# Adapter, layer norm and conditional linear on one core: the squares of the variance read the row sum, not the mean

## The reference

```python
h = relu(x @ W1[lang] + b1[lang])            # 512 -> 128
y = x + h @ W2[lang] + b2[lang]              # 128 -> 512, residual
mean = y.mean(-1); var = ((y - mean) ** 2).mean(-1)
n = (y - mean) * rsqrt(var + 1e-5)
x1 = x + n * gamma[lang] + beta[lang]
out = x1 + x1 @ W[cat] + b[cat]              # 512 -> 512
```

## Time and profile before

| | us |
|---|---|
| median of 3 runs | 620.67 |
| lowest and highest | 618.24, 621.05 |
| the profiled execution | 621.52 |
| its span, first to last instruction | 619.6 |
| PE, DVE, ACT, POOL busy in it | 610.4, 522.8, 510.6, 548.1 |
| granted TensorE clock | 1.000 of full speed |

### The profile page before, as it was taken

The page is one execution under the profiler, slowest core; times in us unless marked ns, Lnnn a source line. Parts: engine busy times, 40 slices in busy tenths (PEclk is TensorE's granted clock), DMA queues, the critical chain, the costliest instruction groups (busy, mean ns, idle before and its releaser), DMA issues.

```text
span 619.6 us, 10902 instructions
## 1 busy us (share of the span) xinstructions
PE 610.4 (99%) x2876; PEld 491.0 (79%) x2876; DVE 522.8 (84%) x1153; ACT 510.6 (82%) x769; POOL 548.1 (88%) x442
## 2 busy tenths in 40 slices
PE   9999999999999999999999999999999999999997
PEld 7667888887878787888787877877878887888786
DVE  1799898888998889898889888889898889898673
ACT  3768888889889889889889888888888889889770
POOL 3689999999999998999999999999999999999930
PEclk9999999999999999999999999999999999999999
DMA  8968998898998888988888997988988898897422
GB/s 299 236 205 277 312 302 286 250 294 261 308 299 272 269 281 268 312 276 295 263 295 261 305 300 246 286 286 270 307 295 274 274 297 253 302 303 264 163 85 103
DMA packets 125616, 166.25 MB, mean 268 GB/s; under 512 B 10866, under 2 KB 72316, under 8 KB 121488
## 3 DMA queue, kind: packets, MB, share of 16 engines
q1 hardware_dynamic: 94612, 150.12, 73.7%
q10 hardware_dynamic: 30972, 15.78, 9.0%
HBM read 132.17 MB, written 33.55 MB: 267 GB/s over the span
## 4 chain that ended last, share of the span: by engine, by line
PE 35%; POOL 29%; ACT 14%; issue 10%; DVE 6%; DMA 3%; SPq 2%; ACTq 1%; POOLq 0%; DVEq 0%
POOL xs_lo L375 8%; ACT norm L473 8%; POOL w_lo L402 7%; PE o_bank L807 7%; PE o_bank L805 6%; PE o_bank L806 6%; POOL x_tok L396 5%; POOL w_raw L386 3%; PE n_bank L823 3%; POOL w_lo L362 3%; DMA b_bc<-in_L_cond_b 2%; PE d_bank L836 2%; PE d_bank L805 2%; PE d_bank L807 2%; PE d_bank L806 2%
## 5 line engine op out<-in xcount | busy, mean ns | idle before, releaser
L805 PE MATMUL o_bank<-w_hi,x1T_hi 128*128 128x512 f32 x512 | 205.7, 402 | 0.9 <-DVE x1T_lo L706 0.8
L807 PE MATMUL o_bank<-w_hi,x1T_lo 128*128 128x512 f32 x512 | 200.5, 392 | 0.0
L806 PE MATMUL o_bank<-w_lo,x1T_hi 128*128 128x512 f32 x512 | 199.6, 390 | 0.0
L396 POOL TENSOR_TENSOR x_tok<-x_tok,b_bc 128x512 f32<-128x512 f32 x128 | 163.8, 1304 | 12.5 <-PE o_bank L885 7.6
L402 POOL TENSOR_TENSOR w_lo<-w_raw,w_hi 128x512 fp32r<-128x512 f32 x128 | 163.3, 1300 | 9.9 <-ACT w_hi L483 9.9
L473 ACT ACTIVATE norm<-y,neg_mean_rstd,rstd 128x512 f32<-128x512 f32 x127 | 151.2, 1267 | 1.1 <-DVE neg_mean_rstd L691 1.1
L641 DVE STREAM_TRANSPOSE xT<-x_quad 128x512 f32<-128x512 f32 x120 | 126.8, 1102 | 29.8 <-DMA x_quad<-in_x 29.8
L807 PEld LDWEIGHTS o_bank<-w_hi,x1T_lo 128*128 128x128 f32 x512 | 96.1, 188 | 21.0
L805 PEld LDWEIGHTS o_bank<-w_hi,x1T_hi 128*128 128x128 f32 x512 | 96.3, 188 | 20.5 <-issue 2.2
L490 ACT ACTIVATE x1T_hi<-n_bank,params 128x512 fp32r<-128x512 f32 x126 | 84.3, 688 | 33.9 <-DVE n_bank L700 19.6
L806 PEld LDWEIGHTS o_bank<-w_lo,x1T_hi 128*128 128x128 f32 x512 | 96.4, 188 | 17.9
(11 more groups left out here) (77 smaller groups left out, 800.0 us busy)
## 6 DMA issues: line engine op xcount, KB each, us to landing
w_raw<-in_L_cond_W SPq DMA_DIRECT2D x32, 1024.0 KB, 6.6
out<-out_half SPq DMA_DIRECT2D x63, 512.0 KB, 4.0
x_tok<-in_x SPq DMA_DIRECT2D x31, 1024.0 KB, 11.2
w_raw<-in_L_cond_W SPq DMA_DIRECT2D x64, 256.0 KB, 4.2
b_bc<-in_L_cond_b SPq DMA_DIRECT2D x64, 256.0 KB, 8.8
x_quad<-in_x SPq DMA_DIRECT2D x62, 256.0 KB, 3.7
x_quad<-in_x ACTq DMA_DIRECT2D x58, 256.0 KB, 10.6
x_tok<-in_x ACTq DMA_DIRECT2D x2, 256.0 KB, 3.2
```

Source lines behind the costliest of these rows:

```text
L396: pool.tensor_tensor(x_tok[p][:, t, :], x_tok[p][:, t, :], b2_bc[p][:, :], ALU.add).then_inc(x_b2_done, 1)
L805: pe.matmul(acc, lhs_hi, rhs_hi, start=first, stop=False)
L806: pe.matmul(acc, lhs_hi, rhs_lo, start=False, stop=False)
L807: return pe.matmul(acc, lhs_lo, rhs_hi, start=False, stop=last)
```

## The change

`mean` and its buffer and semaphore are gone. The square takes the row sum itself as bias and -512 as scale: with H = 512 and s the row sum, (-512 y + s)^2 is 512^2 (y - mean)^2, so the root and the variance divide the sum of squares by 512^3 in place of 512. The square now waits for its `y` tile alone. `variance`, which reads all four sums, has a wait for the `y` tiles that the means had before.

```diff
             def square(k, t):
                 act.wait_ge(y_done, k.count(NT, 0, t + 1))
-                act.wait_ge(mean_done, k.count(NT, 0, t + 1))
-                act.activation(x_tok[k.b][:, t, :], y[:, t, :], ACT.Square, bias=neg_mean[:, t:t + 1],
+                act.activation(x_tok[k.b][:, t, :], y[:, t, :], ACT.Square, scale=-float(H), bias=y_sum[:, t:t + 1],
                                accum_out=sq_sum[:, t:t + 1]).then_inc(sq_done, 1)
             def deviation(k):
-                act.activation(std[:, :], sq_sum[:, :], ACT.Sqrt, scale=1.0 / H,
+                act.activation(std[:, :], sq_sum[:, :], ACT.Sqrt, scale=1.0 / H ** 3,
-            def mean(k, t):
-                dve.wait_ge(y_done, k.count(NT, 0, t + 1))
-                dve.tensor_scalar(neg_mean[:, t:t + 1], y_sum[:, t:t + 1], -1.0 / H, None, ALU.mult
-                                  ).then_inc(mean_done, 1)
             def y_pair(k, i):
                 y_tile(k, 2 * i)
                 y_tile(k, 2 * i + 1)
-                mean(k, 2 * i)
-                mean(k, 2 * i + 1)
             def variance(k):
+                dve.wait_ge(y_done, k.count(NT, 0, NT))
                 dve.tensor_scalar(neg_mean_copy, y_sum[:, :], -1.0 / H, None, ALU.mult).then_inc(stat_done, 1)
                 dve.wait_ge(sq_done, k.count(NT, 0, NT))
-                dve.tensor_scalar(var_eps, sq_sum[:, :], 1.0 / H, EPS, ALU.mult, ALU.add).then_inc(stat_done, 1)
+                dve.tensor_scalar(var_eps, sq_sum[:, :], 1.0 / H ** 3, EPS, ALU.mult, ALU.add).then_inc(stat_done, 1)
             for t in range(NT):
                 y_tile(k0, t)
-                mean(k0, t)
```

More of the change, by code:

```diff
@@ L115, in adapter_then_conditional_linear @@
         y_sum = sb("y_sum", [P, NT])
-        neg_mean = sb("neg_mean", [P, NT])
         sq_sum = sb("sq_sum", [P, NT])
@@ L201, in adapter_then_conditional_linear @@
         y_done = sem("y_done")
-        mean_done = sem("mean_done")
         stat_done = sem("stat_done")
```

## The result

The changed kernel takes 622.18 us (median of 7 runs, 620.35 to 623.70), the kernel before 619.32 (7 runs). The ratio is 1.0046, 95% interval 1.0031 to 1.0062. The forecast was 618.9, in a range of 616.9 to 621.2, and a gain.

A forecast was written before the change was run, and what follows sets the result against it. PE, busy 99% of the span, was taken as the bound, so only its stalls could be won: 1.3 + 0.5 + 0.3 = 2.1 us off 621.52, 619.4 in the profile, 618.9 forecast as the median, range 616.9 to 621.2.

The forecast's parts named there:

- 1.3 + 0.5 + 0.3: Gain in us from fewer late-quad stalls, fewer slow-issue stalls and an earlier end of the last sample: 2.1 together.
- the floor of 18.40 us: PE's own time per sample where nothing is late; 26 steady periods stood 3.84 us above it, all stalls.
- ACT's lead ends at POOL: ACT's 0.45 us lead from earlier squares is lost at its cast of W, which waits for POOL; norms start unchanged.
- SP's train moves ahead: DVE's earlier output tile 3 lets SP issue the next quads and the step's other transfers 0.47 us earlier.
- How much of the head start reaches the landing: Of SP's 0.47 us head start, two thirds, 0.3 us, was taken to reach the landing of the quads DVE awaits.
- How much of the stalls that cancels: In PE's steady part the lead cancels 1.3 of 1.6 us from late quads and 0.5 of 2.2 from slow issues.
- Late quads 1.6, slow issues 2.2: Split of PE's 3.84 us of stalls: DVE waiting for `x_quad`, and ACT's slow issue of two quad transfers before `high_x1`.
- rival 1: All PE stalls go and it runs at its floor: 4.15 us gained, 616.6 to 617.4 as a median; chance 0.19.
- Rival 2: The lead ends at the quads' landing because transfers share DMA; only the end's 0.3 us remains, 620.4; chance 0.24.
- Rival 3: Slower: SP's shifted issues meet ACT's pair of quad issues in more samples, 3.2 us or more, up to 624.7; chance 0.07.
- The start: From the first samples to the first big product, where the second sample waits for POOL's identity: gain 0, bounds 0 and 0.3.
- The end: In the last sample ACT's cast waits for DVE's output tile, so norms and PE's turning come earlier: 0.3 us gained.

The follow-up runs named there:

- e3: The changed kernel with 32 tiny memsets behind DVE's loop, ahead of the last outputs: 622.20 us against 619.68 for the kernel before, ratio 1.0031.
- e1: The changed kernel with 32 tiny memsets on DVE ahead of its loop: 618.48 us against 619.68 for the kernel before, ratio 0.9972.
- e4: The squares' part of the change alone, DVE still making the means, unread: 619.88 us against 619.68 for the kernel before, ratio 0.9998.
- e11: The changed kernel with 160 tiny memsets ahead of DVE's loop: 617.86 us against 620.18 for the kernel before, ratio 0.9956.
- e12: The changed kernel with 48 tiny memsets ahead of DVE's loop, one execution: 618.72 us against 620.18 for the kernel before.
- e2: The kernel before with 88 tiny memsets ahead of DVE's loop: 624.40 us against 619.68 without them, ratio 1.0074.
- e6: The changed kernel with 16 tiny memsets ahead of DVE's loop, one execution: 624.83 us against 619.38 for the kernel before.
- e8: The changed kernel with 32 memsets ahead of DVE's loop, ACT issuing its quads later, behind `high_w2_of_next`: 618.17 us, ratio 0.9985 to the kernel before.
- e9: The changed kernel with 100 tiny memsets ahead of DVE's loop, one execution: 622.96 us against 619.48 for the kernel before.

## Why the prediction was wrong, point by point

- **The step that failed** is the sum itself: it priced the removed instructions by their time and by what that lead reaches, 1.3 + 0.5 + 0.3, and put what DVE's loop pays at its two jumps back at nothing, without a reason. DVE's program got shorter, and its loop moved within it. The missing term is worth +3.7 us (e3 against e1, same chip), and turns -1.2 (e1 against before) into a loss. The slower rival was another mechanism, SP's issues against ACT's; the upper end of the range, 621.2, left no room for this one.
- *The bound by PE's starts, and the floor of 18.40 us*: right. All periods without a stall have it within 0.03 us, in every kernel.
- *The means are worth 0.47 us of DVE a sample*: right. From the first `y` tile to `x1(2)` it took 330.67 - 327.75 = 2.92 us, and takes 332.24 - 329.80 = 2.44 now. The `y` tiles follow each other without a gap, 0.61 us apart, and `x1(2)` starts right behind the last one:

```profile
331.02 0.68 DVE L652 SCALAR_TENSOR_TENSOR y<-y_bank,x_tok 128x512 f32<-128x512 f32 x1
...
331.63 0.69 DVE L652 SCALAR_TENSOR_TENSOR y<-d_bank,x_tok 128x512 f32<-128x512 f32 x1
...
332.24 1.41 DVE L691 SCALAR_TENSOR_TENSOR n_bank<-n_bank,params,xT 128x512 f32<-128x512 f32 x2
```

- *The squares cost the same with a scale*: right. 0.71 us where 0.72, and no idle time ahead of the first. *ACT's lead ends at POOL*: right; its cast now waits longer for POOL (timeline of ACT after, where 0.85 stood in the earlier trace rows), and e4 finds nothing:

```profile
330.72 0.71 ACT L506 ACTIVATE x_tok<-y,y_sum 128x512 f32<-128x512 f32 x1
...
336.75 1.06 ACT L481 ACTIVATE w_hi<-w_raw 128x1024 fp32r<-128x1024 f32 x1 [1.34 <-POOL w_raw L384]
```

- *SP's train moves ahead*: right. SP's quads now start at 320.86 in the sample that PE begins at 321.52, 0.66 ahead of it, where they stood at PE's start before (300.38 and, by PE's row there, 300.34). Over 24 samples the quads start 0.09 us ahead of PE on average before, 0.14 in e4, 0.61 in the changed kernel and 0.63 in e1:

```profile
320.86 0.90 SPq L229 DMA_DIRECT2D x_quad<-in_x  x2
```

- *How much of the head start reaches the landing*: more than the two thirds that were taken. DVE's first transposition of a sample starts on average 1.34 us ahead of PE's start before, 1.36 in e4 and 1.95 in e1, with ACT's issues at the same place in the period, so the whole lead arrives.
- *How much of the stalls that cancels*: 1.45 us in the steady part of e1 (3.84 to 2.39), where the sum had 1.8; in e11 2.91, in e12 2.36. The parts of the sum came out otherwise in e1: the stalls that are not behind a slow pair of issues went from 1.85 to 0.43 us (1.3 was taken), those behind a slow pair stayed, 1.99 and 1.96 (0.5 was taken). In e11 they are 0.87; how many pairs are slow differs from execution to execution (in e4, which has the means, 1.25 us are behind slow pairs and 2.21 are not).
- *Late quads 1.6, slow issues 2.2*: about right for the execution that was read, if the 1.99 us behind slow pairs are counted as theirs. Both causes can be at work in one late period, and no run takes them apart.
- *The time from which the gain is taken*: luck is in it. The profiled execution before, 621.52 us, is 2.2 above the median of the seven runs, 619.32, and the 620.67 of three runs was 1.35 above it. Without its stalls it would have taken 621.52 - 3.84 = 617.7, so that a median run has, as an estimate, 1.6 us of stalls in the steady part and not 3.84. The profiled executions of the kernel before and of e1 differ by 2.1 us (621.52 and 619.44), as the sum had it; the medians differ by 1.2, 0.7 to 2.8 by the interval. That e1's 618.48 lies so near to the forecast 618.9 is in part due to these two errors. (In the first rival 3.84 + 0.3 is 4.14, not 4.15.)
- *The rivals*: some stalls stay in each kernel with the issues on ACT (e1, e11, e12), so rival 1 is out. Rival 2, that the lead ends at the landing, is out by the landing times above and by e1 against e4. Rival 3 is out as well: pairs of 1.3 us or more are seven in the trace before and four in e4's, two in the changed kernel's, four in e1's and two in e11's.
- *The start*: 0 was forecast, and the changed kernel lost 0.56 us by 97.15 (96.59 before). In its trace quads land at 59.45 us, 2.3 us later than before, which may be the cause. e1 and e3 have 96.65 and 96.42 there, so it belongs to that execution. *The end*: from the last sample's start to the end of the span 40.17 us in the changed kernel, 40.77 before; 0.6 gained where 0.3 was forecast. But e4 and e2, which have the means, take 40.51 and 40.45, so that 0.3 to 0.6 is what the traces show.

## What to carry to other kernels

Removing or adding instructions on an engine with a loop moves the loop in its program, and a jump back can then cost some microseconds of fetching, which the diff of the work doesn't show: here 2.9 to 3.7 us for two jumps, more than the edit gains. Before judging a small edit, look at each jump for idle time put down to nothing, and at the number of instruction packets; then try the edit with a few cheap instructions in front of the loop, in more than one number, since 32 cured it here and 16 and 100 did not. And where a ring has no slack, a transfer's issue belongs on an engine off the ring: that alone gave 0.38%, about what the edit gave in a good place (0.28% and 0.44%), and with it the edit gave nothing more. Last, a profile is one execution: before its stalls are taken as what can be won, set its time against the median.

## What the runs showed of the hardware

- A jump back of DVE that misses costs 3.8 to 5.0 us of idle time (12 jumps in 6 kernels), and up to 1.6 us more a few instructions later (e6). PE has 616 instructions in its loop. A second instruction queue, which I take for PE's, has 11 packets of 16384 bytes in the changed kernel's trace, none from 252.7 to 612.2 us; no engine but DVE has idle time of this kind at a jump in the lists of waits.
- In two pairs of places 128 instructions apart the outcome is the same, and the packets of queue 14 have 8192 bytes. A loop of 304 instructions from place 302 makes its second and third pass without a packet; one of 280 from 270, 286, 370 or 398, or of 304 from 390, doesn't.
- Two transfers issued by ACT take 0.9 us, but up to 2.0 us in some samples of the kernel before and 2.23 in e1, at a time when SP issues too. With the changed kernel the second quad issue of SP took 1.62 and 1.48 us in the samples at 152.4 and 226.5 us in place of 0.35, with a packet of that second instruction queue starting less than 0.5 us before. In e1, e3, e6, e8, e9, e11 and e12 each issue of SP's first quads of 0.99 us or more in the steady part has such a packet less than 0.5 us ahead too. Whether the one causes the other was not tried.
